# Experts' rows turned into two PSUM banks and split in halves, with an earlier second expert load and base rows added one per expert

## The reference

```python
sh_mid = gelu(einsum('th,ehd->ted', xt, Wsh_up))        # 2 shared experts, D = 256
shared_out = einsum('ted,edh->th', sh_mid, Wsh_down)
probs = softmax(xt @ W_router)                           # 16 routed experts
top_v, top_i = top_k(probs, 2)
gate = sum(one_hot(top_i, 16) * top_v[..., None], axis=1)
rt_mid = gelu(einsum('th,ehd->ted', xt, Wrt_up))
routed_out = einsum('ted,edh->th', rt_mid * gate[:, :, None], Wrt_down)
x = x + gb * (shared_out + routed_out)
```

## Time and profile before

| | us |
|---|---|
| median of 3 runs | 929.03 |
| lowest | 927.0 |
| highest | 1271.75 |
| profiled execution | 921.43 |
| its span, first to last instruction | 919.7 |
| TensorE busy in it | 887.2 |
| granted TensorE clock in it, mean | 0.99 |

### The profile page before, as it was taken

One profiled execution on the slowest core, in us unless ns is written; L12 is line 12 of the kernel. 1 busy time (PEld: TensorE's weight loads), 2 busy tenths in 40 slices (PEclk: granted clock), 3 DMA queues, 4 the chain that ended last, 5 costly groups with the idle time before them and its releaser, 6 DMA issues.

```text
span 919.7 us, 13596 instructions
## 1 busy us (share of the span) xinstructions
PE 887.2 (96%) x4264; PEld 715.2 (78%) x4265; DVE 502.7 (55%) x967; ACT 402.0 (44%) x688; POOL 384.2 (42%) x282
## 2 busy tenths in 40 slices
PE   6899989999998999999999999999999999999996
PEld 2367778788776888888888888888887887888875
DVE  4685999884847111454135513651496444444388
ACT  3575875875645432322232223225444333333352
POOL 3231120100022546226202530258537699998473
PEclk9899999999999999999999999999999999999998
DMA  9659577654155328396214321466435788775787
GB/s 357 218 176 307 167 244 253 204 185 135 49 189 201 114 92 274 119 288 212 92 34 158 118 92 35 154 218 212 161 115 195 244 255 264 271 272 207 250 248 192
DMA packets 122401, 174.07 MB, mean 189 GB/s; under 512 B 8792, under 2 KB 70232, under 8 KB 119280
## 3 DMA queue, kind: packets, MB, share of 16 engines
q1 hardware_dynamic: 59472, 111.58, 35.5%
q0 software_dynamic: 9216, 34.61, 12.1%
q10 hardware_dynamic: 53664, 27.26, 10.3%
HBM read 97.60 MB, written 75.83 MB: 189 GB/s over the span
## 4 chain that ended last, share of the span: by engine, by line
PE 84%; ACT 5%; DMA 4%; DVE 3%; issue 2%; POOL 1%; SPq 0%; ACTq 0%; DVEq 0%
PE kk_ps L427 6%; PE kv_ps L427 6%; PE kk_ps L429 6%; PE kv_ps L429 6%; PE kk_ps L428 6%; PE kv_ps L428 6%; PE mm_ps L427 6%; PE mm_ps L428 6%; PE mm_ps L429 6%; PE up_ps L427 4%; PE dn_ps L427 3%; PE dn_ps L429 3%; PE dn_ps L428 3%; PE up_ps L428 3%; PE up_ps L429 3%
## 5 line engine op out<-in xcount | busy, mean ns | idle before, releaser
L1576 DVE TENSOR_TENSOR silu<-kk_ps,silu 128x512 fp32r<-128x512 f32 x64 | 44.3, 691 | 199.9 <-ACT silu L2266 199.6
L2262 ACT ACTIVATE kk_ps<-kk_ps 128x512 f32<-128x512 f32 x64 | 37.2, 582 | 206.8 <-PE kk_ps L429 206.8
L427 PE MATMUL kk_ps<-xk,cm_w 128*128 128x512 f32 x256 | 100.9, 394 | 0.0
L427 PE MATMUL kv_ps<-cm_w,silu 128*128 128x512 f32 x256 | 100.5, 393 | 0.0
L429 PE MATMUL kk_ps<-xk,cm_w 128*128 128x512 f32 x256 | 99.8, 390 | 0.0
L429 PE MATMUL kv_ps<-cm_w,silu 128*128 128x512 f32 x256 | 99.7, 390 | 0.0
L428 PE MATMUL kk_ps<-xk,cm_w 128*128 128x512 f32 x256 | 99.6, 389 | 0.0
L428 PE MATMUL kv_ps<-cm_w,silu 128*128 128x512 f32 x256 | 99.6, 389 | 0.0
L2439 POOL TENSOR_TENSOR rs<-mv,neghalf 128x4 f32<-128x4 f32 (+2 forms) x13 | 15.8, 1217 | 152.6 <-DVE mv L1327 139.9
L2432 POOL TENSOR_TENSOR cm_w<-stage,cm_w 128x1024 fp32r<-128x1024 f32 x16 | 38.7, 2422 | 91.1 <-ACT cm_w L2026 72.3
L2490 POOL TENSOR_TENSOR rs<-mv,neghalf 128x1 f32<-128x1 f32 x16 | 16.1, 1008 | 127.4 <-DVE mv L1601 127.4
(11 more groups left out here) (306 smaller groups left out, 2345.9 us busy)
## 6 DMA issues: line engine op xcount, KB each, us to landing
xs_s<-zero ACTq DMA_DIRECT2D x13, 1024.0 KB, 7.9
ys_s<-zero ACTq DMA_DIRECT2D x13, 1024.0 KB, 6.3
xsb<-xs_s SPq DMA_DIRECT2D x44, 256.0 KB, 3.7
ys_s<-ysb SPq DMA_DIRECT2D x41, 256.0 KB, 4.1
ex_raw<-in_wex POOLq DMA_DIRECT2D x9, 1024.0 KB, 6.7
stage<-in_wcm SPq DMA_DIRECT2D x16, 512.0 KB, 3.7
wmod<-in_wmod SPq DMA_DIRECT2D x6, 1024.0 KB, 11.7
ex_raw<-in_wex SPq DMA_DIRECT2D x6, 1024.0 KB, 7.2
```

Source lines behind the costliest of these rows:

```text
L427: pe.matmul(out, lhs[0], rhs[0], start=first, stop=False)
L1576: dve.tensor_tensor(silu[:, g % NSILU, 1, :], kk_ps[g % 2][:, :], silu[:, g % NSILU, 0, :].bitcast(F32), ALU.subtract).then_inc(s_silo, 1)
L2262: act.activation(kk_ps[g % 2][:, :], kk_ps[g % 2][:, :], ACT.Silu).then_inc(s_silu, 1)
```

## The change

- `turn_x` puts transposes k = 0, 1 into bank `xs_ps[0]` and k = 2, 3 into `xs_ps[1]`, each bank holding a half of both parities, and counts `s_tx` up after each half, so twice a tile. SP's and TensorE's thresholds on `s_tx`, `s_txhi` and `s_txlo` are doubled.
- `turned_hi` and `turned_lo` work in two instructions of 256 columns, with a wait and a count each.
- `up` waits for the first half ahead of k = 0 and for the second ahead of k = 2.
- Ahead of the loop, `turn_x(1)` stands behind the nine matmuls of `shared_down`, with a wait for both halves of tile 0.
- `expert_split` counts up `s_exr` by the difference itself. Its wait for that difference and the separate count are gone.
- `expert_load(5)` stands ahead of `expert_split(4)`; `expert_load(6)` stands behind `expert_split(5)`.
- `base_add` is made once after each of experts 5 to 12.

```diff
@@ load_xs
-                    sp.wait_ge(s_tx, wait)
+                    sp.wait_ge(s_tx, wait * 2)
@@ shared_up
-                            pe.wait_ge(s_txhi, pairs * 2 + 2)
-                            pe.wait_ge(s_txlo, pairs * 2 + 2)
+                            pe.wait_ge(s_txhi, pairs * 4 + 4)
+                            pe.wait_ge(s_txlo, pairs * 4 + 4)
@@ turn_x
                 for k in range(KT):
-                    mm = pe.transpose(xs_ps[par][:, k, :], xsb[:, par, k * P:(k + 1) * P], ident[:, :])
-                mm.then_inc(s_tx, 1)
+                    mm = pe.transpose(xs_ps[k // 2][:, par * 2 + k % 2, :], xsb[:, par, k * P:(k + 1) * P], ident[:, :])
+                    if k % 2:
+                        mm.then_inc(s_tx, 1)
@@ up
                 pe.wait_ge(s_exr, word)
-                pe.wait_ge(s_txlo, count)
                 for k in range(KT):
+                    if k % 2 == 0:
+                        pe.wait_ge(s_txlo, count * 2 - 1 + k // 2)
@@ ahead of TensorE's loop
             turn_x(0, 16)
+            shared_down(1, [3], first)
+            pe.wait_ge(s_txlo, 2)
             turn_x(1, 16)
-            shared_down(1, [3], first)
@@ turned_lo
-                dve.wait_ge(s_txhi, count)
-                dve.tensor_tensor(xsT[:, par, 1], xs_ps[par][:, :, :], xsT[:, par, 0].bitcast(F32), ALU.subtract)\
-                    .then_inc(s_txlo, 1)
+                for h in range(2):
+                    dve.wait_ge(s_txhi, count * 2 - 1 + h)
+                    dve.tensor_tensor(xsT[:, par, 1, h * 2:h * 2 + 2], xs_ps[h][:, par * 2:par * 2 + 2, :],
+                                      xsT[:, par, 0, h * 2:h * 2 + 2].bitcast(F32), ALU.subtract).then_inc(s_txlo, 1)
@@ turned_hi
-                act.wait_ge(s_tx, count)
-                act.activation(xsT[:, par, 0], xs_ps[par][:, :, :], ACT.Copy).then_inc(s_txhi, 1)
+                for h in range(2):
+                    act.wait_ge(s_tx, count * 2 - 1 + h)
+                    act.activation(xsT[:, par, 0, h * 2:h * 2 + 2], xs_ps[h][:, par * 2:par * 2 + 2, :], ACT.Copy)\
+                        .then_inc(s_txhi, 1)
@@ expert_split
-                n = 2 * (e - PRE)
+                n = e - PRE
                 pool.tensor_tensor(hi, raw_of(e), zero[:, 0:1].to_broadcast([P, UNIT]), ALU.add).then_inc(s_exd, 1)
                 pool.wait_ge(s_exd, n + 1)
-                pool.tensor_tensor(lo, raw_of(e), hi.bitcast(F32), ALU.subtract).then_inc(s_exd, 1)
-                pool.wait_ge(s_exd, n + 2)
-                pool.sem_inc(s_exr, 8)
+                pool.tensor_tensor(lo, raw_of(e), hi.bitcast(F32), ALU.subtract).then_inc(s_exr, 8)
@@ GpSimd's order
             ht_lo(2)
+            expert_load(PRE + 1)
             expert_split(PRE)
-            expert_load(PRE + 1)
 
             for e in range(PRE + 1, NE):
-                if e + 1 < NE:
+                if PRE + 1 < e < NE - 1:
                     expert_load(e + 1)
                 expert_split(e)
-                if e <= PRE + TT:
-                    base_add(2 * (e - PRE - 1))
-                    base_add(2 * (e - PRE - 1) + 1)
+                if e == PRE + 1:
+                    expert_load(e + 1)
+                if e <= PRE + SB * TT:
+                    base_add(e - PRE - 1)
```

## The result

The changed kernel is slower by half a per cent: 932.74 us against 927.94 us, medians of 17 runs each; the ratio, without the one execution of before that took 1271.75 us, is 1.0054 with a 95% interval of 1.0041 to 1.0068. The forecast was 924.3, half a per cent faster, with a range up to 931. The profiled execution took 934.63 us, its span is 932.8 (before: 921.43 and 919.7).

What follows compares the result with a forecast made beforehand. TensorE was taken to bound the kernel, idle 8.5 us ahead of `up`. The terms 8.5 - 2.6 - 1.0 - 0.25 gave 4.7 us less, so 929.03 - 4.7 = 924.3 us, range 917.5 to 931.

Steps and rivals of the forecast that it cites:

- Halves, two banks: Ahead of `up`: TensorE no longer waits for `s_txlo`, which cost 0.25 us a tile in 37 tiles; 8.5 us gained.
- rival (d): Fixed cost per instruction makes halves no faster, so `up` in effect waits for both; 927.7 us, chance 0.05.
- The second threshold and the sequencer: TensorE's sequencer in the loop: slow reads of the next expert's word give back about 1.0 us (bounds 0 and 3).
- Transfers that set the pace: Row loads and `ysb` stores in the loop: landings fixed after issue give back 2.6 us (bounds 0 and 5).
- rival (e): Slower: GpSimd becomes the bound at expert 13, and bursts cost one more landing; 931 us, chance 0.13.
- Prologue: Ahead of the loop: ScalarE's second copy delays the GELU table load and the first GELU; 0.25 us lost.
- Experts: GpSimd's loads and splits: expert 13 ready at about 822.8, 5.1 us earlier; GpSimd keeps ahead by some 3 us.
- The tail shifts whole: After the loop: gathers wait for stores of `ysb`, which move with TensorE, so nothing is added.

Runs made afterwards that it cites:

- experiment 6: The changed kernel unaltered, measured again beside the kernel before on another chip; 931.22 against 925.06 us, ratio 1.0090.
- experiment 10: The changed kernel with four one-element additions on GpSimd ahead of the gather loop; ratio 1.0051 to the kernel before.
- experiment 2: The kernel before with only GpSimd's part of the change (load order, spread base adds, no wait on the last split); ratio 1.0049.
- Experiment 3: The changed kernel with the base adds in pairs again, over four experts; ratio 1.0008 to the kernel before.
- experiment 12: The changed kernel with the old order of expert loads, base adds in pairs and the `gb2` loads behind the expert loop; 924.51 us, ratio 0.9967.
- experiment 11: The changed kernel with the four `gb2` broadcast loads moved behind the expert loop; 929.88 us, ratio 1.0047 to the kernel before.
- experiment 15: The changed kernel with each base add cut to 16 of 128 partitions, expert loads whole, outputs incomplete; ratio 0.9941 to the kernel before.
- experiment 7: The changed kernel with each expert load from expert 7 on as two transfers of 512 KB; ratio 0.9994 to the kernel before.
- experiment 9: The kernel before with four one-element additions on GpSimd ahead of the gather loop; ratio 1.0032 to the kernel before.
- experiment 14: The changed kernel with expert loads from expert 5 on cut to 16 of 128 partitions (128 KB), outputs wrong; ratio 0.9928 to the kernel before.
- experiment 8: The changed kernel with GpSimd's part as before, but expert loads from expert 7 on in two 512 KB transfers; ratio 1.0009 to the kernel before.
- experiment 16: The kernel of experiment 12 with each expert load from the seventh on in two 512 KB transfers; 921.64 against 925.41 us before, ratio 0.9954.

## Why the prediction failed, step by step

**Halves, two banks: right.** The "issue" time fell by 7.5 us to 1.0 ("under 2"), the pitch to 3.48 ("about 3.5"). All of the gate's 0.26 a tile was gained, 10.2 over the loop. The halves cost what the earlier trace rows said; in the groups by line of the changed kernel, 712 to 863 (busy us, mean ns):

```profile
L1907 DVE TENSOR_TENSOR xsT<-xs_ps,xsT 128x256 fp32r<-128x256 f32 x75 | 28.6, 420 | 55.4 <-ACT xsT L2354 55.4
L2354 ACT ACTIVATE xsT<-xs_ps 128x256 fp32r<-128x256 f32 x76 | 25.2, 385 | 12.0 <-PE xs_ps L1190 11.9
```

VectorE sat idle 55.4 us ahead of these, so the fixed share of an instruction, on which rival (d) and the page VectorE: DVE Perf Modes of the Trainium skill rested, fell on idle time, as weighed.

**The second threshold and the sequencer: right in size.** 1.0 us of "issue" is left ahead of `up`, as was set for it, and 1.0 ahead of `mb`'s turning, where the kernel before had 0.6. Two figures of this part were loose and changed nothing: the second half is 0.6 us early by the prediction's own times (715.5 against 715.39 and 0.7), not 0.9, and 830.2 less three quarters of 4.7 is 826.7, not 826.

**Transfers that set the pace: the step that failed.** It put 2.6 us, with a bound of 5, for what late rows and stores would give back. Late rows cost 10.6 us more than before, and the slow clock behind them 6.8, 17 in all by the first pair of profiles (by the others the waits are 10.7 and 11.5 against 3.1 to 3.7, the slow clock 3.4 each, against 1.7 in one profile of before). Three things were wrong in it. First, "a landing comes at a fixed time after its issue" took the landings of before as given, and only counted the earlier need (0.48 for two tiles; measured, 6.6 us from issue to need became 6.1). But the change also altered who else is on the DMA engines at that time. Before, the slowest row load took 7.3 to 8.8 us in four profiles; with GpSimd's part of the change it took 9.0 to 9.7, whether the rows were turned in halves (after, experiments 6 and 10) or not (9.4 in experiment 2). With the turning alone it took 7.9. The profile of before had the 8.1 already, 1.5 us over the time to the need; that slow landings could get slower was left out of the estimate. Second, the bound of 0 "if thinner bursts of base rows calm the queue" had the sign wrong: one base add beside each of eight expert loads makes bursts of 1.25 MB eight times (two of them larger, with expert 6's load and with `gb2`) in place of 1.5 MB four times. Experiment 3 points to the cost of spreading them, 12 against 11 shows it together with that of the new order, and experiment 15 that of having them there at all. Third, it had no term for the clock, which it named only as a thing that would make it wrong. The burst at 737 to 741 was even seen, in rival (e), and priced at 0.7 us. It cost 4.7 at tile 11 (pitch 8.22 less 3.48) and 1.0 at the next (4.48).

**Prologue: nearly.** `up` of tile 1 came 3.17 after that of tile 0, against 2.75: 0.42 lost, 0.25 predicted.

**Experts: right up to expert 6, then late by what the stall gave it.** The last split of an expert ended at 728.75, 737.06 and 752.59 for experts 4, 5 and 6 (predicted 728.6, 737 and 752.4). Expert 7's came 13.2 us later, at 765.83 (predicted 9.8 later), those of 8 to 12 every 9.9. Expert 13 ended at 827.33, not 822.8. In GpSimd's timeline of the changed kernel:

```profile
752.52 0.89 POOL L2568 DMA_DIRECT2D base<-x_s  x1
756.72 0.18 POOL L2554 TENSOR_TENSOR thr<-zero 128x1 f32<-128x1 f32 x1 [3.31 <-PE dn_ps L429]
...
815.85 2.43 POOL L2591 DMA_DIRECT2D gb<-mod_s  x4
...
822.75 4.58 POOL L2563 TENSOR_TENSOR ex_w<-ex_raw,ex_w 128x2048 fp32r<-128x2048 f32 x1
```

GpSimd waits 3.31 us for the last `down` of expert 3, which the stall at tile 11 had delayed; that is most of the 4.5. It never held TensorE: tile 32 begins `up` at 839.59. So the time lies just above the 931 of rival (e), but not by its mechanism; experiment 7 shows that mechanism, at the price of 4.8 us at tile 32 and 2.4 at the next, which ran at the lower clock, in a kernel whose rows are on time.

**The tail shifts whole: neither shown nor refuted.** The first pair of profiles differs by 6 us there; a third of before has 63.0 itself. Between kernels with the same disturbance on one chip 0.4 to 2.5 us are left (63.4 to 65.4 against 63.0 on chip 1), unexplained. On chip 10 before had no disturbance and the three others had it, 4.5 to 4.9 us apart.

**The balance in the measured time.** By the loops of the profiles (after 154.9, 151.2 and, with the additions of experiment 10, 152.7; before 148.1, 149.0, 150.0 and, with those of experiment 9, 150.4) the change costs 3.6 us on the mean, 152.9 less 149.4, and 0.4 in the prologue: 4.0, beside the 4.8 us between the medians. With loops that differ by 2 to 4 us from profile to profile of one kernel this is no proof, and on chip 10 it doesn't come out: 2.3 and 0.4 beside 6.2. What is missing there would have to be in the last stage.

## What to carry to other kernels

When a change shortens the pitch of a loop or moves transfers, list for every load that feeds it the time from issue to need, and what else is issued in the microseconds around it; price it by its slowest landing beside such a burst, not by the median. A gain on the engine that sets the pace and a spreading of background transfers can each look free and together take the last margin. Take a large background transfer apart before making the engine faster, and check that its consumer has the slack for it.

## What the runs showed of the hardware

- A 256 KB row load on SyncE's queue with nothing issued on GpSimd's queue from 9 us before it to 4 after landed in 2.5 to 2.8 us in 14 of the 19 cases that the profiles time, and in 3.3 to 4.5 in the rest. Beside a 1 MB load and a base add on GpSimd's queue the slowest took 7.3 to 8.8 in the kernel before and 9.0 to 9.7 in the changed one. The queues are apart; the 16 DMA engines aren't (share 1.01 at 333 GB/s in the window 741 to 748). The Trainium skill, DMA: Bandwidth & Descriptors, in its section on queues, rings and completion order, says that each DMA engine takes the queues it has work for in turn, a packet at a time. That fits experiments 14 and 15, where late rows held TensorE for 1.2 and 5.1 us with less on the other queue; no run here varied the packets.
- The stall of 3.0 us at tile 11 was followed by 6.8 us at a granted clock of 0.5 and cost 4.7 us there and 1.0 at the next tile. Waits of 1.8 (experiment 10) to 5.2 us (experiment 8) were met or followed by 3.4 to 6.8 us of it, but not every one: four of 2.2 to 2.9 us (experiments 3, 6, 8 and 11) were not, nor was any in experiments 12, 14 and 16, none over 1.9 us.
- In the last stage a gather that takes GpSimd 0.96 us took 2.8 to 3.4 us at three places, in seven profiles on two chips, the kernel before among them. In nine others ScalarE, VectorE and SyncE stood still together, by VectorE's timeline for 2.0 to 2.3 and then 5.0 to 7.6 us, while GpSimd went on with its gathers; the kernel before with four additions is among these. Only two profiles, both of before, have neither. What sets either off is not settled; a kernel compared by one profile each can be wrong by 5 us in this stage.

The long gathers in the timeline of the third profile of before:

```profile
886.03 2.77 POOL L2595 DMA_INDIRECT g1b<-ys_s,spos  x1 [0.30 <-issue]
886.69 1.29 DVE L1961 TENSOR_TENSOR g1b<-g1b,base 128x512 f32<-128x512 f32 x2
887.89 1.41 DVE L1946 SCALAR_TENSOR_TENSOR g1b<-g2b,gates,g1b 128x512 f32<-128x512 f32 x2
889.10 3.44 POOL L2595 DMA_INDIRECT g1b<-ys_s,spos  x1 [0.30 <-issue]
889.22 1.29 DVE L1955 TENSOR_TENSOR g1b<-g1b,gb 128x512 f32<-128x512 f32 x2
890.42 1.29 DVE L1961 TENSOR_TENSOR g1b<-g1b,base 128x512 f32<-128x512 f32 x2
891.62 1.41 DVE L1946 SCALAR_TENSOR_TENSOR g1b<-g2b,gates,g1b 128x512 f32<-128x512 f32 x2
```

Each lasts while VectorE works without a break on pairs of SBUF tiles, and ends in a SCALAR_TENSOR_TENSOR (the third, 892.85 to 896.27, has one instruction with a PSUM input among them). The Trainium skill, GPSIMD Engine Reference, Specifications, says that GpSimd shares its SBUF interfaces with VectorE and contends with instructions that have two SBUF inputs. These rows agree with it, but no run here took VectorE's work away to show it.
